# A graph network layer on one core: the first four groups gathered from the raw input, the last node update moved into the build banks, the end's loads issued earlier

## The reference

```python
h = jnp.maximum(_layernorm(x, axis=-1), 0.0)
x = x + _L0_gnn_ref(h, edge_index, edge_attr_64, W1, b1, W2, b2, U1, c1, U2, c2)
h = jnp.maximum(_layernorm(x, axis=-1), 0.0)
x = x + _L1_gnn_ref(h, edge_index, edge_weight)

def _L0_gnn_ref(node_features, edge_index, edge_features, W1, b1, W2, b2, U1, c1, U2, c2):
    msg_input = jnp.concatenate([node_features[src], edge_features], axis=-1)
    h = jax.nn.relu(msg_input @ W1 + b1)
    aggregated = jax.ops.segment_sum(h @ W2 + b2, dst, num_segments=6250)
    g = jax.nn.relu(jnp.concatenate([node_features, aggregated], axis=-1) @ U1 + c1)
    return g @ U2 + c2

def _L1_gnn_ref(x, eidx, enorm):
    return jax.ops.segment_sum(x[src] * enorm[:, None], dst, num_segments=6250)
```

## Time and profile before

| what | us |
|---|---|
| median of 3 runs | 2261.81 |
| profiled execution, its own time | 2270.83 |
| its span on the core | 2269.0 |
| POOL busy | 1613.5 |
| PE matmul busy | 1797.8 |
| DVE busy | 1632.2 |

### The profile page before, as it was taken

The page is one execution under the profiler, slowest core; times in us unless marked ns, Lnnn a source line. Parts: engine busy times, 40 slices in busy tenths (PEclk is TensorE's granted clock), DMA queues, the critical chain, the costliest instruction groups (busy, mean ns, idle before and its releaser), DMA issues.

```text
span 2269.0 us, 52026 instructions
## 1 busy us (share of the span) xinstructions
PE 1797.8 (79%) x19448; PEld 1527.7 (67%) x19448; DVE 1632.2 (72%) x4933; ACT 842.8 (37%) x1470; POOL 1613.5 (71%) x1671
## 2 busy tenths in 40 slices
PE   6766576767677777778778877888888899999898
PEld 6555455655565666567667766776777788788787
DVE  7876677767776777777777777777777677877564
ACT  5333343434343434333343333434334333433211
POOL 7777777777777777777777777777777777777200
PEclk9988889878998999899989999999999999999999
DMA  4355556555764676378548755875876588578798
GB/s 104 113 179 178 179 176 204 185 172 173 241 208 137 197 249 209 112 232 255 187 129 260 247 159 165 255 227 156 248 234 197 170 268 257 154 218 255 228 304 278
DMA packets 375605, 459.58 MB, mean 203 GB/s; under 512 B 77256, under 2 KB 297688, under 8 KB 371766
## 3 DMA queue, kind: packets, MB, share of 16 engines
q1 hardware_dynamic: 317274, 401.51, 53.7%
q0 software_dynamic: 51776, 53.07, 10.3%
q10 hardware_dynamic: 6300, 1.60, 0.3%
HBM read 281.45 MB, written 174.54 MB: 201 GB/s over the span
## 4 chain that ended last, share of the span: by engine, by line
POOL 67%; issue 21%; PE 8%; DMA 3%; DVE 1%; ACT 0%; SPq 0%; POOLq 0%
POOL rows L780 67%; PE pair L1266 2%; PE pair L1046 1%; DMA stage<-tail 1%; DMA late_piece<-adjacency 1%; PE pair L1162 1%; PE pair L1290 1%; PE pair L1180 1%; PE pair L1147 1%; PE pair L1280 1%; DMA stage<-adjacency 0%; PE pair L1034 0%; PE pair L1298 0%; DMA rows<-table,idx 0%; PE pair L1272 0%
## 5 line engine op out<-in xcount | busy, mean ns | idle before, releaser
L780 POOL DMA_INDIRECT rows<-table,idx x1616 | 1574.2, 974 | 494.6 <-issue 492.4
L906 ACT COPY stage<-pair 128x600 f32<-128x600 f32 x808 | 538.7, 667 | 882.3 <-PE pair L1147 837.7
L1147 PE MATMUL pair<-bld 128*128 128x300 bf16 x4848 | 757.6, 309 | 5.7 <-DVE bld L1599 5.6
L1147 PEld LDWEIGHTS pair<-bld 128*128 128x128 bf16 x4848 | 549.0, 118 | 140.9 <-issue 14.0
L1599 DVE TENSOR_SCALAR bld<-iota_key,key 128x300 bf16<-128x300 f16 x1616 | 583.0, 361 | 78.1 <-PE pair L1147 75.9
L1609 DVE TENSOR_TENSOR bld<-bld,part 128x512 bf16<-128x512 bf16 x1212 | 481.6, 397 | 0.0
L1107 PE MATMUL pair<-w1b,rings 128*128 128x128 f32 x1616 | 258.2, 310 | 253.3 <-DVE rings L1575 252.9
L1575 DVE TENSOR_TENSOR rings<-rows,pair 128x512 f32<-128x512 f32 x202 | 138.9, 688 | 427.9 <-DMA rows<-table,idx 424.4
L1107 PEld LDWEIGHTS pair<-w1b,rings 128*128 128x128 f32 x1616 | 227.6, 216 | 289.0 <-DVE rings L1575 286.6
L1180 PE MATMUL pair<-late_piece,h 125*64 125x192 f32 x1856 | 201.9, 337 | 117.2 <-issue 104.6
L1162 PE MATMUL pair<-stage,h 125*64 125x96 f32 x4230 | 234.8, 253 | 0.2 <-issue 0.2
(11 more groups left out here) (155 smaller groups left out, 1120.8 us busy)
## 6 DMA issues: line engine op xcount, KB each, us to landing
late_piece<-adjacency SPq DMA_DIRECT2D x232, 480.0 KB
rings<-in_edge_attr_dram SPq DMA_DIRECT2D x202, 256.0 KB
adjacency<-stage SPq DMA_DIRECT2D x14, 2160.0 KB
rows<-table,idx POOLq DMA_INDIRECT x1616
tail<-stage SPq DMA_DIRECT2D x101, 240.0 KB
stage<-tail SPq DMA_DIRECT2D x50, 480.0 KB, 5.8
adjacency<-stage SPq DMA_DIRECT2D x10, 1920.0 KB
adjacency<-stage SPq DMA_DIRECT2D x10, 1680.0 KB
```

Of the source, the lines that this page charges most:

```text
L780: pool.indirect_dma_start(out=rows[:, slot, t, :], out_offset=None, in_=table, in_offset=bass.IndirectOffsetOnAxis(ap=idx[:, g, t:t + 1], ...
L906: act.copy(tiles[:, g % STAGE, :, 2 * j * WT:2 * (j + 1) * WT].rearrange("p h (o w) -> p o h w", w=WT), build_pair[i % 2][:, :, 0:KEYS].re ...
L1147: last = pe.matmul(build_pair[i // 2 % 2][:, t % 2, 0:KEYS], hot_w[q % 2][k][:, :, u], hot_key[q % 2][:, u, :], start=(k == 0), stop=(k == ...
```

## The change

1. **Raw rows.** For groups 0 to 3 (RAW = 4) POOL gathers rows of the input x itself. Their indices come straight from `src` by two DMAs on ACT's queue. DVE and ACT normalise the gathered edge rows as the preamble does the nodes (`centre_raw`, `variance_raw`, `normalise_raw`, `square_raw`, `root_raw`), PE turns them (`turn_raw`), ACT keeps them (`keep_raw`), and PE multiplies them by w1a and adds b1 in the same bank as the edge product (`make_raw_q`). `add_fast` then copies instead of adding.
2. **Room and lead.** Groups 0 to 18 (EARLY = 19) get buffers of their own in memory that is idle then (`late_piece`, `h2`, part of `nodes`). Up to group 21 POOL waits for the landing of group g - 3, and from group 9 on also for `pre_made` at g - LEAD + 1, LEAD = 9, which says that group g - 9 was consumed. From group 22 on the ring's wait is as before. The gathers after group 5 stand inside the branch on `fast`. ACT clears the borrowed part of `nodes` in groups 20 to 24.
3. **Preamble.** POOL drops the blanking of `nodes`, the cast and the `hi` passes. ACT blanks (`fill_rows`) and casts; DVE does the `hi` passes and some small memsets; ACT keeps the eight key and rel tables that DVE kept.
4. **Last update.** `make_g` and `make_up` of chunk 9 go to the banks that the tiles were built in, directly after group 201's first half of `direct` and ahead of batch 100's `direct` and group 201's `late`. DVE and ACT follow in that order.
5. **End's loads.** SP waits only for what quads 0 to 3 need before it loads them; the other waits come behind those loads. Pieces use the slots shifted by five.

```diff
+RAW = 4
+IN_H2 = 6
+EARLY = 19
+BOTH = 6
+LEAD = 9
...
+        def flat_rows(g):
+            if g < RAW:
+                return late_all[:, g * ROWS:(g + 1) * ROWS]
+            if g < RAW + IN_H2:
+                return h2_all[:, (g - RAW) * ROWS:(g - RAW + 1) * ROWS]
+            at = N + HELD + (g - RAW - IN_H2) * ROWS
+            return nodes[:, at:at + ROWS]
...
+            def fast_gather(g):
+                if g >= EARLY + RING:
+                    pool.wait_ge(pre_made, g - RING + 1)
+                elif g >= RING:
+                    landed(g - RING)
+                    if g >= LEAD:
+                        pool.wait_ge(pre_made, g - LEAD + 1)
+                gather(x if g < RAW else table1, g, rows_of(g))
...
-            pool.wait_ge(consts_set, 14)
-            pool.wait_ge(iotas_set, 2)
-            pool.wait_ge(ones_set, CHUNKS)
+            pool.wait_ge(idx_loaded, 32)
+            for g in range(RAW):
+                fast_gather(g)
             pool.wait_ge(kept_act, 4)
             for s in range(2):
                 pool.wait_ge(t1_stored[s], 16 * CHUNKS // 2)
-            for g in range(GROUPS):
-                gather1(g)
-            pool.wait_ge(pre_made, GROUPS)
+            for g in range(RAW, BOTH):
+                fast_gather(g)
             pool.wait_ge(fast_made, 2)
             fast = pool.value_load(fast_i[0:1, 0:1], min_val=0, max_val=1)
             with pool.If(fast > 0):
-                pool.nop()
+                for g in range(BOTH, GROUPS):
+                    fast_gather(g)
+                pool.wait_ge(pre_made, GROUPS)
...
+            act.dma_start(idx[:, 0, :], src[E - GE:E].rearrange("(p t) -> p t", t=T)).then_inc(idx_loaded, 16)
+            act.dma_start(idx[:, 1:RAW, :], src[0:(RAW - 1) * GE].rearrange("(g p t) -> p g t", p=P, t=T)
+                          ).then_inc(idx_loaded, 16)
...
+            def make_raw_q(g, slot, bank):
+                wait_step(pe, eaT_kept, g)
+                pe.wait_ge(raw_act, after_raw(RAW_ACT, "kept", g))
+                for a in range(T // 2):
+                    to = bank[:, a * P:(a + 1) * P]
+                    pe.matmul(to, eaT[:, slot, a, :], w1b2[:, :], start=True, stop=False)
+                    pe.matmul(to, e_turned_kept[:, a, :], w1a2[:, :], start=False, stop=False)
+                    for i in range(2):
+                        last = pe.matmul(to[:, i * D:(i + 1) * D], ones[D:D + 1, :], w1a[D:D + 1, :], start=False,
+                                         stop=(i == 1))
+                last.then_inc(q_made, 1)
...
+            def centre_raw(g):
+                of = rows_of(g)
+                gathered_wait(dve, g, g % RING, 0)
+                dve.tensor_reduce(e_sum[:, :], of, AX_X, ALU.add).then_inc(raw_dve, 1)
+                dve.wait_ge(raw_dve, after_raw(RAW_DVE, "summed", g))
+                dve.tensor_scalar(e_mean[:, :], e_sum[:, :], 1.0 / D, None, ALU.mult).then_inc(raw_dve, 1)
+                dve.wait_ge(raw_dve, after_raw(RAW_DVE, "mean", g))
+                dve.tensor_tensor(of, of, spread(e_mean[:, :], D), ALU.subtract).then_inc(raw_dve, 1)
...
             def fast_groups():
-                for s in range(GROUPS + 6):
+                centre_raw(0)
+                make_quad(0)
+                variance_raw(0)
+                normalise_raw(0)
+                make_quad(1)
+                for s in range(GROUPS):
...
+                    if s + 1 < RAW:
+                        centre_raw(s + 1)
...
+                add_sums(GROUPS - 1)
+                add_up(FINAL, final_up[0:NP, 0:BC])
+                centre(2)(FINAL, 0)
+                variance(2)(FINAL, 0)
+                stage_h2(FINAL, 0)
...
+                    if s == GROUPS - 1:
+                        make_g(FINAL, 0)
+                        make_g(FINAL, 1)
+                        direct(BATCHES - 1, 0)
+                        make_up(FINAL)
+                        direct(BATCHES - 1, 1)
                     late(s)
...
             def fast_end():
+                final = BATCHES - 1
+                store_adjacency(final)
+                store_partial(final - 1)
+                tiles_stored((final - 1) % 2)
+                for q in range(AHEAD):
+                    load_quad(q)
+                store_partial(final)
+                for n, c, q in LATE_AT[GROUPS - 1]:
+                    store_late(n, q)
+                tiles_stored(final % 2)
+                for q in range(AHEAD, ENDS):
+                    load_quad(q)
```

More of the change, by code:

```diff
@@ L616, in load_late @@
             def load_late(n, c, q, fresh):
+                if n == 0:
+                    sp.wait_ge(pre_made, RAW)
                 if fresh:
@@ L773, in _, with gather @@
-            for h in range(2):
-                n = HALF[h]
-                pool.wait_ge(hi_made, h + 3)
-                pool.tensor_scalar(hi_g[0:n, h, :], hi_g[0:n, h, :], -ROUND, None, ALU.add).then_inc(hi_made, 1)
-            def gather(table, g, slot):
+                      allow_small_or_imprecise_dtypes=True).then_inc(consts_set, 1)
+            def gather(table, g, to):
                 for t in range(T):
                     pool.indirect_dma_start(
-                        out=rows[:, slot, t, :], out_offset=None, in_=table,
+                        out=to[:, t, :], out_offset=None, in_=table,
@@ L787, in gather1 @@
                     pool.wait_ge(pre_made, g - RING + 1)
-                gather(table1, g, g % RING)
+                gather(table1, g, rows[:, g % RING, :, :])
             def gather2(g):
@@ L806, in _ @@
             with pool.If(fast > 0):
-                pool.nop()
+                for g in range(BOTH, GROUPS):
+                    fast_gather(g)
+                pool.wait_ge(pre_made, GROUPS)
             with pool.Else():
+                for g in range(BOTH - RING, BOTH):
+                    landed(g)
+                for g in range(GROUPS):
+                    gather1(g)
+                pool.wait_ge(pre_made, GROUPS)
                 for s in range(2):
@@ L847, in keep, with sources_as_f32, fill_rows, clear @@
                 act.wait_ge(table_turned, j + 1)
[L848 to L849 removed]
+                act.copy(to[:, g0 + skip:g0 + n, 4 * q:4 * q + 4],
+                         pair[3][:, j % 2, :].rearrange("p (t g) -> p g t", g=P)[:, skip:n, :]).then_inc(kept_act, 1)
+            def sources_as_f32():
+                act.wait_ge(src_loaded, 80)
+                for h in range(2):
+                    n = HALF[h]
+                    act.copy(src_f[0:n, h, :], src_i[0:n, h, :]).then_inc(src_made, 1)
+            def fill_rows(c, slot):
+                act.activation(nodes[D:DEG + 1, c * CN:(c + 1) * CN],
+                               ones[D:DEG + 1, 0:1].to_broadcast([DEG + 1 - D, CN]), ACT.Copy,
+                               scale=fill[D:DEG + 1, 0:1]).then_inc(ones_set, 1)
             def keep_sources():
                 for j in range(4):
[L853 to L861 removed]
+                    keep(j, idx, RAW if j < 2 else 0)
+            def clear(first, last, cleared):
+                act.activation(sums1[:, first:last], ones[:, 0:1].to_broadcast([P, last - first]), ACT.Copy,
+                               scale=0.0).then_inc(cleared, 1)
+            held_pieces = [HELD + (HELD_END - HELD) * i // 5 for i in range(6)]
+            def clear_held(i):
+                clear(held_pieces[i], held_pieces[i + 1], sums_cleared)
+            unrolled(CHUNKS, ((1, root(1)), (0, square(1)), (0, fill_rows), (2, stage_hT), (3, stage_t1)),
+                     {8: sources_as_f32, 10: keep_sources})
+            for first, last in ((0, CN), (CN, HELD), (HELD_END, N + W)):
+                clear(first, last, sums_cleared)
             for j in range(4, 8):
@@ L878, in _ @@
             last.then_inc(cols_kept, 1)
+            for j in range(12, 16):
+                keep(j, key)
+            for j in range(16, 20):
+                keep(j, rel)
             def keep_eaT(g, slot, bank):
@@ L1224, in fast_groups @@
                 turn_ea(1, 1, ea_bank)
-                make_q(0, 0, q_bank)
-                for s in range(GROUPS + 6):
+                turn_raw(0)
+                make_raw_q(0, 0, q_bank)
+                for s in range(GROUPS):
                     if s < GROUPS:
```

326 lines of the change are left out of this document (202 added, 124 removed).

## The result

The changed kernel took **2227.38 us** (median of 4 runs, 2226.27 to 2230.35) against 2262.19 for the kernel before (4 runs). The ratio is 0.9841, 95% interval 0.9829 to 0.9853: 34.8 us faster. The forecast was 2217, so the sign and the main mechanism held, and about 10 us of the gain of 44 are missing. The time lies outside the forecast's own range of 2209 to 2225 and inside the stated one, up to 2229, only because that took in the first two rivals.

What follows compares the result with a forecast made beforehand. POOL's row of gathers was taken to bound the kernel; a start 38.7 us earlier and a tail 5.5 us shorter took the median 2261.8 by 44.2 to 2217 us, own range 2209 to 2225, stated range 2209 to 2229.

Steps and rivals of the forecast that it cites:

- the first two rivals: Raw groups too slow for the consumers (2220 to 2228 us, chance 0.10); raw gathers stretched (2228 us, chance 0.11).
- What bounds the kernel: Whole span: POOL's row of 1616 gathers sets the time; only an earlier start or shorter tail helps.
- Term 1: Start: group 4's gathers begin at about 49.5 us, 49.2 us earlier, once raw gathers and table1 are done.
- the step on the table: Preamble: without POOL's blanking the chunks come nearly 3 us earlier; table1 lands at 49.2, at worst 2 us later than before.
- Term 2: Gathers after group 4's start: DVE work, the branch and catching up give back 10.5 us, leaving 38.7 us earlier.
- Term 3: Consumers of raw groups: about 12 us each, group 19 reached at 238, so gather 22 at 243.5 needn't wait.
- eight of one row come on top: Raw product on PE: eight products of 128 columns take 2.5 us; the one-row ones were given no time.
- the first rival: Raw groups too slow for the consumers: gather 22 waits 3 to 10 us, time 2220 to 2228; chance 0.10.
- Term 4: Tail: the last node update is covered by other products and PE's clock stays up: minus 5.5 us, bounds 2 and 8.
- Dearer gathers in the branch: Rival, gathers from group 6 on: each costs more; at 50 ns each the time is 2295 us; chance 0.03.
- Stretched raw gathers: Rival, the 32 raw gathers: beside DVE's work each takes 1.68 us, group 4 starts at 60, time 2228; chance 0.11.
- the prediction's own signs: Timeline checks: right if group 4 starts at 48 to 52 without waiting at gather 22; wrong if raw gathers far exceed 1.3.

Runs made afterwards that it cites:

- the first experiment: Changed kernel with b1 added by VectorE, SyncE's weight loads behind the table stores, and VectorE's whole-number passes earlier: 2221.32 us, ratio 0.9810.
- The kernel with the second queue: Kernel of the first experiment, with ScalarE issuing the table stores of odd chunks on its own queue: 2223.11 us, ratio 0.9802; on slow chips 3130.70 us, 1.0091.

## Why the prediction was right, and where not

- **What bounds the kernel**: right. POOL's row of gathers moved forward and the whole kernel with it.
- **Term 1, group 4 at 49.5**: 5.05 us too early, the first of two steps that failed. The first raw gather came at 4.83 (6 was forecast), and the 32 took 46.1 us (42.5), up to 50.95. What failed is the step on the table: I let it follow from the node chain alone and took its landing, 3 us behind the last block, from a row in which the queue had caught up. I had left out of the preamble's transfers the raw gathers' 23 to 26 GB/s and how long the index loads fill the DMA engines ahead of the stores. The two weight loads more on SP's queue, which I had left out too, matter little: with all eleven behind the table it gained 0.64 us. The table landed near 54, not at 49.2 or, at worst, 52.4.
- **Term 2, 10.5 us given back**: 7.1 (16.6 less the wait of 9.53); which of its parts was too high wasn't tried. Together with the wait the start brings 27.5 us at group 22 (282.16 - 254.68) in place of 38.7.
- **Term 3, the consumers**: wrong. The step is "eight of one row come on top", taken as next to nothing beside the eight products of 128 columns. They cost 4.2 us a group. The eight full products were too cheap as well: the 1616 of the earlier trace rows are instructions, two for each of 808 products, so 0.31 us is one instruction's, and eight products aren't 8 x 0.31 = 2.5 us. They took 3.55 us alone and 4.6 beside the one-row ones. With 16.5 us a group on the mean instead of 12 and a first group added at 90.16, not 87, group 19 was added at 253.72, not 238, and POOL waited 9.53 us. This is the first rival, to which 0.10 was given, with the price that it named (3 to 10 us). The two runs without these products show the cause.
- **Term 4, the tail**: mechanism right, 7.9 us in the profile and 6.6 alone in the median for 5.5. From group 201's `direct` to the end's first product PE needs 11.25 us instead of 16.06, 4.8 less for the 4.5 forecast. The third quad's first product then starts 2.15 us behind the first one's, where it was 4.29 at the low clock: 2.1 us, for which I had put 1 to 1.5 and kept a part for the loads.
- **Dearer gathers in the branch**: no. From group 19 on 965 ns and 0.30 us each; before it was 974 ns over all gathers.
- **Stretched raw gathers**: in part. Many took 1.21 us and one 4.08, so they came 1.44 us apart, between the 1.33 that the 42.5 us amount to and the rival's 1.68. That cost 3.6 us of POOL's time against the forecast but none of the kernel's, since the table came last.
- The sum: -5.05 (table) - 9.53 (wait) + 3.4 (less given back) + 2.4 (tail) = -8.8 us, which takes the forecast's 44.2 to 35.4; measured 34.8. By the prediction's own signs the first raw gather (4.83, near 5 to 7), the last gather (2081.54, near 2079) and PE's vanished pause came out right, while group 4's start (54.55, not 48 to 52), POOL at gather 22 (9.53 us of waiting) and the spacing of the raw gathers (1.44, above 1.3) were its signs of being wrong. That the sum still fell within 10 us is the work of terms that erred to both sides.

## What to carry to other kernels

Price a product by its instructions and by the columns of weights it loads, not by its depth: here a bias as a one-row product in f32 cost about what a full one costs, while VectorE, which must read the bank anyway, took 0.69 us with the bias added and 0.69 us for the bare copy. When work is taken off a critical engine's path, ask for the next thing in line by its transfers, not only by its compute: here the table's stores. And read a gain in a profiled execution by stretches: one that the change doesn't touch tells how much of the difference is scatter.

## What the runs showed of the hardware

- A product one row deep and 64 columns wide in f32 took 0.52 us, one 128 deep and 128 wide 0.56 beside it and 0.43 among its like. In the first block of group 1 the two full ones took 0.30 and 0.32 us and the two one-row ones 0.96 together.
- The raw gather of 4.08 us ended at 50.95, and DVE's six passes ran from 47.14 to 50.83, 0.6 us apart and with no gap; the gather ended 0.12 us behind the last. The Trainium skill ("SBUF — State Buffer", SBUF: two separate sides, the trap of DVE blocking a DMA) says that a VectorE operation in a two-port mode keeps GpSimd from writing descriptors until it ends; this row agrees, if these passes run in such a mode, which no row shows. But in the first experiment the same six passes ran from 33.14 to 37.2, in a row too, and the gathers beside them took 0.95, 1.02, 1.02 and 1.02 us, while single passes took up to 0.81 instead of 0.68 us, as if the engines took turns. What decides between the two is open.
- 256 B pieces: 90 GB/s for one stream, 105 to 110 with the raw gathers beside it, at 0.40 and 0.48 of the DMA engines' time.
- The same kernel takes 2262 us on some chips and 3104 to 3152 on others, at a granted clock of 0.931 and 0.807. The kernel with the second queue, which ran on both kinds, was 2.0% faster than before on the first and 0.9% slower on the other; the changed kernel itself ran only on the first.
